# The projection of the condition with its weights streaming 512 wide, h with the batch on partitions, and u flipped back on TensorE

## What is computed

```python
u = gelu(cond @ W_proj + b_proj, approximate=False)          # 128 x 512
logits = (u @ W_u)[:, None, :] + einsum('bnd,dc->bnc', x, W_e)
out = x + logits                                              # 128 x 128 x 512
```

## Time and profile before

| | |
|---|---|
| median of 3 runs | 380.01 us (376.68, 380.01, 381.04) |
| profiled execution, span | 375.2 us |
| its own time beside the span | not listed; the three listed runs lie 1.5 to 5.9 us above the span |
| PE busy | 366.5 us (98%) |
| DVE, POOL, ACT busy | 213.6, 153.0, 75.9 us |
| mean granted TensorE clock | 0.995 |

### The profile page before, as it was taken

One profiled execution on the slowest core, in us unless ns is written; L12 is line 12 of the kernel. 1 busy time (PEld: TensorE's weight loads), 2 busy tenths in 40 slices (PEclk: granted clock), 3 DMA queues, 4 the chain that ended last, 5 costly groups with the idle time before them and its releaser, 6 DMA issues.

```text
span 375.2 us, 4431 instructions
## 1 busy us (share of the span) xinstructions
PE 366.5 (98%) x1617; PEld 303.4 (81%) x1617; DVE 213.6 (57%) x204; ACT 75.9 (20%) x78; POOL 153.0 (41%) x72
## 2 busy tenths in 40 slices
PE   5997999999999999999999999999999999999997
PEld 3896888888888888888888888888888888888886
DVE  2553697556655655665566556556655665565322
ACT  3243132211221221122122212211221222122100
POOL 2022376345435534543454355345434533543400
PEclk9899999999999999999999999999999999999999
DMA  7999669985949498593939769393966939322223
GB/s 217 313 202 200 132 179 284 240 278 106 242 144 230 174 180 268 109 268 120 244 153 188 259 121 270 114 257 132 201 246 129 288 96 250 132 112 112 112 96 129
DMA packets 71206, 70.59 MB, mean 188 GB/s; under 512 B 1953, under 2 KB 65697, under 8 KB 66977
## 3 DMA queue, kind: packets, MB, share of 16 engines
q1 hardware_dynamic: 71200, 70.53, 74.2%
HBM read 36.96 MB, written 33.55 MB: 188 GB/s over the span
## 4 chain that ended last, share of the span: by engine, by line
PE 89%; SPq 6%; DMA 3%; DVE 1%; issue 0%
PE banks L424 30%; PE banks L425 30%; PE banks L426 30%; SPq L166 4%; DMA x_raw<-in_x 3%; SPq L188 1%; DVE x_t L297 1%; SPq L177 0%; SPq L174 0%; SPq L186 0%; SPq L185 0%; DVE u_lo L348 0%; SPq L184 0%; DVE y L373 0%
## 5 line engine op out<-in xcount | busy, mean ns | idle before, releaser
L242 POOL TENSOR_TENSOR x_lo<-x_t,x_hi 128x1024 fp32r<-128x1024 f32 x62 | 149.6, 2413 | 194.1 <-ACT x_hi L274 194.1
L424 PE MATMUL banks<-w_hi,x_hi 128*128 128x512 f32 (+1 forms) x508 | 197.0, 388 | 0.0
L426 PE MATMUL banks<-w_hi,x_lo 128*128 128x512 f32 (+1 forms) x508 | 196.8, 387 | 0.0
L425 PE MATMUL banks<-w_lo,x_hi 128*128 128x512 f32 (+1 forms) x508 | 196.8, 387 | 0.0
L315 DVE TENSOR_TENSOR y<-banks,bias 128x1024 f32<-128x1024 f32 x63 | 77.0, 1223 | 131.3 <-PE banks L426 131.3
L297 DVE STREAM_TRANSPOSE x_t<-x_raw 128x512 f32<-128x512 f32 x124 | 130.3, 1105 | 10.6 <-DMA x_raw<-in_x 10.6
L274 ACT CAST x_hi<-x_t 128x1024 fp32r<-128x1024 f32 x62 | 65.5, 1056 | 260.8 <-PE banks L426 238.7
L426 PEld LDWEIGHTS banks<-w_hi,x_lo 128*128 128x128 f32 x508 | 95.4, 188 | 19.6
L424 PEld LDWEIGHTS banks<-w_hi,x_hi 128*128 128x128 f32 x508 | 95.4, 188 | 19.5
L425 PEld LDWEIGHTS banks<-w_lo,x_hi 128*128 128x128 f32 x508 | 95.4, 188 | 19.3
L444 PEld LDWEIGHTS banks<-cond_t,w_proj_sb 128*128 128x128 f32 x32 | 7.5, 328 | 0.0
(11 more groups left out here) (32 smaller groups left out, 36.1 us busy)
## 6 DMA issues: line engine op xcount, KB each, us to landing
out<-y SPq DMA_DIRECT2D x31, 1024.0 KB, 4.3
x_raw<-in_x SPq DMA_DIRECT2D x61, 512.0 KB, 8.7
w_e<-in_L_cond_weight_matrix SPq DMA_DIRECT2D x4, 256.0 KB, 5.4
w_proj_sb<-in_L_cond_W_proj SPq DMA_DIRECT2D x1, 1024.0 KB, 11.2
x_raw<-in_x SPq DMA_DIRECT2D x8, 128.0 KB, 8.8
w_u<-in_L_cond_weight_matrix SPq DMA_DIRECT2D x1, 1024.0 KB, 12.7
x_raw<-in_x SPq DMA_DIRECT2D x2, 256.0 KB, 2.9
out<-y SPq DMA_DIRECT2D x1, 512.0 KB, 2.6
```

What stands on the lines that cost most here:

```text
L242: pool.tensor_tensor(x_lo[s][:, :, :, :], x_t[s][:, :, :, :], x_hi[s][:, :, :, :].bitcast(F32), ALU.subtract).then_inc(lo_ready, 1)
L424: pe.matmul(bank, a_hi[:, j, :], b_hi[:, j, cols], start=(j == 0), stop=False)
L425: pe.matmul(bank, a_hi[:, j, :], b_lo[:, j, cols], start=False, stop=False)
L426: last = pe.matmul(bank, a_lo[:, j, :], b_hi[:, j, cols], start=False, stop=(j == NJ - 1))
```

## The change

The projection is issued as four float32 matmuls with a block of `cond_t` stationary and W_proj's rows moving, 512 columns each, so that h has the batch on the partitions. b_proj then runs along the free dimension: it is loaded broadcast to all 128 partitions (2 KB each, 256 KB where it was 2 KB), and DVE adds it out of PSUM into `h`, between the transposes of chunk 3 and `w_u_lo`. ACT applies the gelu in one instruction, `h` to `u`. PE flips `u` back into `cond_psum` after chunk 2, four transposes. ACT's `u_hi` and DVE's `u_lo` read the PSUM tile; `u_hi` stands behind `hi` of chunk 3 now. `u_t` goes away; `h`, `u` and the wide `b_proj_sb` are new, and so are the semaphores `h_summed` and `u_flipped`.

```diff
-    b_proj_dram = b_proj.rearrange("(p j) -> p j", j=NJ)
+    b_proj_rows = b_proj.unsqueeze(0).to_broadcast([P, D])
...
-        b_proj_sb = sb("b_proj_sb", [P, NJ])
+        b_proj_sb = sb("b_proj_sb", [P, D])
+        h = sb("h", [P, D])
+        u = sb("u", [P, D])
...
-        u_t = sb("u_t", [P, NJ, B])
...
-        h_psum = banks[N_BANKS - 1][:, 0, :].rearrange("p (e b) -> p e b", e=NJ)
+        h_psum = banks[N_BANKS - 1][:, 0, :]
...
-            sp.dma_start(b_proj_sb[:, :], b_proj_dram).then_inc(b_proj_loaded, 16)
+            sp.dma_start(b_proj_sb[:, :], b_proj_rows).then_inc(b_proj_loaded, 16)
...
             act.wait_ge(h_ready, 1)
-            act.wait_ge(b_proj_loaded, 16)
-            for e in range(NJ):
-                last = act.activation(u_t[:, e, :], h_psum[:, e, :], ACT.Gelu, bias=b_proj_sb[:, e:e + 1])
-            last.then_inc(u_ready, 1)
-            act.wait_ge(u_ready, 1)
-            act.copy(u_hi[:, :, :], u_t[:, :, :]).then_inc(u_hi_ready, 1)
+            act.activation(u[:, :], h[:, :], ACT.Gelu).then_inc(u_ready, 1)
             for c in range(3, N_SPLIT):
                 hi(c, c, True)
+            act.wait_ge(u_flipped, 1)
+            act.copy(u_hi[:, :, :], cond_psum).then_inc(u_hi_ready, 1)
...
                 else:
+                    dve.wait_ge(b_proj_loaded, 16)
+                    dve.wait_ge(h_summed, 1)
+                    dve.tensor_tensor(h[:, :], h_psum, b_proj_sb[:, :], ALU.add).then_inc(h_ready, 1)
                     dve.wait_ge(w_u_hi_ready, 1)
...
             dve.wait_ge(u_hi_ready, 1)
-            dve.tensor_tensor(u_lo[:, :, :], u_t[:, :, :], u_hi[:, :, :].bitcast(F32),
+            dve.tensor_tensor(u_lo[:, :, :], cond_psum, u_hi[:, :, :].bitcast(F32),
                               ALU.subtract).then_inc(u_lo_ready, 1)
...
-            w_proj_cols = w_proj_sb[:, :, :].rearrange("p j (d e) -> p j e d", e=NJ)
-            for e in range(NJ):
-                for j in range(NJ):
-                    last = pe.matmul(h_psum[:, e, :], w_proj_cols[:, j, e, :], cond_t[:, j, :],
-                                     start=(j == 0), stop=(j == NJ - 1))
-            last.then_inc(h_ready, 1)
+            for j in range(NJ):
+                last = pe.matmul(h_psum, cond_t[:, j, :], w_proj_sb[:, j, :], start=(j == 0), stop=(j == NJ - 1))
+            last.then_inc(h_summed, 1)
...
+            pe.wait_ge(u_ready, 1)
+            flip(cond_psum, u[:, :], u_flipped)
             pe.wait_ge(w_u_hi_ready, 1)
             pe.wait_ge(w_u_lo_ready, 1)
             pe.wait_ge(u_hi_ready, 1)
```

More of the change, by code:

```diff
@@ L124, in build_cond_residual @@
         cond_ready = sem("cond_ready")
+        h_summed = sem("h_summed")
         h_ready = sem("h_ready")
+        u_flipped = sem("u_flipped")
         u_ready = sem("u_ready")
```

## The result

The changed kernel takes 380.2 us (median of 20 runs) against 377.2 us for the kernel before in 20 runs beside it; the ratio is 1.0057, 95% interval 1.0034 to 1.0080. It is slower by about 2.1 us, which is also the distance of the means; the medians lie 3.0 us apart. One of the 20 runs of the changed kernel took 1306 us and is left out of the ratio. The 380.01 us of the table ahead was the median of three runs, and a high one. The profiled execution has a span of 377.2 us where the one before had 375.2.

What follows compares the result with a forecast made beforehand. PE's restart was taken to be bound by slot 1's landing and u_lo, PE otherwise binding. PE's -3.8 + 0.6 counted 0 in a stall; DMA +0.7, clock +1.2 on the 380.0 median gave 381.9 us, range 377.6 to 384.6.

Steps and rivals of the forecast that it cites:

- What bounds the kernel: Before 37.50 us PE waits 2.2 us for u_lo, late through slot 1's load; from 45 us PE itself binds.
- the projection: On PE ahead of chunk 2: four wide matmuls take 3.7 us instead of 7.50, so PE gets through 3.8 earlier.
- the flip: Four transposes of u on PE after chunk 2: 0.63 us added, ending at 32.4, inside the stall.
- PE's restart: Start of the product with W_u, released by u_lo after slot 1 lands: moves from 37.5 to 38.2 us.
- The b_proj term: The 256 KB load ahead of slot 1 in the DMA queue delays its landing and PE's restart: +0.7 us.
- Rival (d): The broadcast reads slowly, 128 reads of the same 2 KB, costing 2.6 us: 383.8 us; chance 0.06.
- The clock: PE's stall before W_u grows to 5.8 us and may bring a half-clock stretch: +1.2 us, bounds 0 and 3.4.
- Rival (a): After PE's restart the clock stays at half for two stretches of 3.4 us: 384.1 us; chance 0.14.
- The sum: PE's saving inside a stall 0, DMA +0.7, clock +1.2: span 375.2 becomes 377.1; on the 380.0 median, 381.9 us.
- How the numbers follow: Differences under one per cent (3.8 us) cannot be told; slower 0.19, beyond one per cent faster 0.06, the rest 0.75.
- Rival (b): Slot 1 usually lands before PE finishes chunk 2, so the projection's saving shows: 376.8 us; chance 0.10.
- (c): The projection on PE gets no shorter (7.5 us), the gap stays near 2 us, the clock stays: 380.7 us; chance 0.10.

Runs made afterwards that it cites:

- before_bcast: The kernel before with one more broadcast load of b_proj (256 KB) into a spare tile nobody reads; 380.9 us, ratio 1.0025 to the kernel before.
- group 1: First of three groups of kernels timed beside the kernel before, to be compared within a group; the kernel before took 377.7 us there.
- small_bias: The changed kernel with b_proj loaded as before (2 KB), DVE adding one number per partition; 378.8 us, ratio 1.0019 to the kernel before.
- twice: The changed kernel with its projection computed twice over (8 matmuls); 378.6 us, ratio 1.0014 to the kernel before.
- after_ulo_first: The changed kernel with DVE's u_lo moved ahead of its wait for slot 1; 373.6 us, ratio 0.9897 to the kernel before.
- fill_gap: The changed kernel with 20 unneeded matmuls of zeros on PE behind the flip of u; 379.6 us, ratio 1.0037 to the kernel before.
- changed again: The changed kernel, unmodified, timed and profiled once more beside the kernel before; 381.0 us, ratio 1.0048, profiled span 379.7 us.

## Why the prediction was right or wrong

**What bounds the kernel, the projection, the flip, ACT and DVE: right.** The restart is ended by `u_lo` behind slot 1's landing; the projection cost 3.59 us for 3.7, the flip 0.63, the gelu 0.63 for 0.65, `u_hi` 0.59, and none of it reached the chain. FP8 and Floating Point Precision of the Trainium skill (TensorE Precision Notes) gives true FP32 four passes through the array. The trace fits that: the weight loads of the eight records start 0.43 us apart in the timeline, near twice a split-precision record's 0.23, so a matmul of two records takes about four times 0.23; the passes themselves it doesn't show. The gain of the projection was 0, as forecast.

**PE's restart: right in kind.** Forecast 38.2, in the two profiles 37.9 and 40.0. The stall was forecast at 5.8 us and was 4.6 and 7.5. The b_proj term was 0.7; the two profiles' landings moved by 0.4 and 2.6, of which a slow spell of the queue has its share, and the means by 0.9. Rival (d), that a broadcast reads more slowly than its bytes, turned out true with four of them and is open for one. I had given it 0.06.

**The clock: right in kind, too small.** I took 1.2 us. The profiled execution lost 1.6, and over all runs the clock's loss is 2.6 us larger than before (4.7 - 2.1), part of which falls on the stall itself. Rival (a), two stretches of half clock, came about in the second profile (6.8 us at 0.50, of which 2.0 us were lost). TensorE: Matmul & The Clock Gate of the Trainium skill (Why this matters for your kernels) warns of idle gaps between bursts. The trace agrees: here the stall of 4.6 us was followed by 3.4 us at half clock, and the one of 7.5 by a clock of 0.50 from 37.5 to 44.3. But behind 2.2 us the clock held in the kernel before, and behind 2.0 us it fell in before_bcast.

**The sum and its base.** The sum gave +1.9 us, and the measured one is +2.1. That near hit has some luck in it: in the profiled pair the b_proj term was too large by 0.3 and the clock's too small by 0.4. The 381.9 us were 1.7 too high all the same, because I added the sum to the median of three runs, 380.0, where twenty gave 377.2. The runs listed with a span lie 1.7 to 1.8 us above it, so the profiled execution before took about 377.0, and not the 380.0 to which I tied its span.

**The verdict: wrong.** I read +1.9 us as no change, with a chance of 0.75 for "within one per cent" and 0.19 for slower. The failing step is the last one, "How the numbers follow": from a spread of 4.4 us over three runs I took it that nothing under 3.8 us could be told. Twenty runs on either side told 0.57% with an interval of 0.23% either way. The spread itself was a clue, as part of it is the clock: of 31 runs of the kernel before (group 1), the ten with a mean clock of 0.991 or less average 380.3 us, the other twenty-one 377.3. That is more than the 1.7 us of one stretch, so something else varies with it; the landing is a candidate, and that isn't shown. I put the clock at 0 for the kernel before. In fact about a third of its runs have a mean clock that fits a second stretch, and in before_bcast's profile that stretch lies behind the old stall. Rival (b), a thinner cover, shows in no profile (slot 1 never landed before 34.6 us), and (c), a projection that gets no shorter, is refuted by its row.

## What to carry to other kernels

Before making an operation in front of a stall faster, ask what ends the stall; if it is a transfer, the saving becomes idle time, and here the longer idle stretch of TensorE also made a low clock behind it more frequent. Look for what merely stands in program order behind the late transfer without needing it: moving one subtraction by DVE ahead of a wait was worth 0.9% in the old kernel, more than the whole projection. And broadcast loads in a full queue can cost more than their bytes (four of them did; for one it isn't shown): a single row and a matmul over a contraction of one did the same for 1.05 us of TensorE. Before calling a small change invisible, take more than three runs: their median was 2.8 us off here.

## What the runs showed of the hardware

- A float32 matmul of 512 columns takes two records that start 0.43 us apart, 0.86 us; one of 128 columns 0.47 us (7.50 / 16). For the same columns the wide form takes less than half the time (3.59 for 7.50).
- A float32 matmul with a contraction of 1 (the row of b_proj) took no less than one of 128: 1.05 us from its start to that of the next.
- The granted clock fell to 0.50 for 3.4 us behind stalls of 4.6 (changed), 4.0 (small_bias), 3.0 (twice) and 2.0 us (before_bcast), and did not behind 2.2 (before), 1.5 (after_ulo_first) and 1.2 us (fill_gap). Behind 7.5 us (changed again) it was 0.50 for 6.8 us, and had fallen 2.5 us before PE worked again.
- The clock column of a profile can read 1.00 where there is no record yet: in the changed kernel's, matmuls run at the spacing of the half clock to about 14 us.
- Four broadcasts of one 2 KB row held the queue at 152 GB/s; with three of them replaced by loads of 128 different rows it moved 304 at the same place.
- The landing of the 2 MB of slot 1 varies between 35.2 and 37.3 us over two profiled executions of one program; in the later one the queue fell to 119 GB/s for 2 us.
